# Moving the transfers of SyncE's queue to GpSimd in a streaming adjacency matmul with residual and layernorm

## The reference, cut to what matters

```
def _L0_gnn_ref(X, A_hat, w, W_agg):
    agg = A_hat @ (X @ W_agg)
    aggregated_term = w[:, None] * jax.nn.relu(agg)
    residual_term = (1.0 - w)[:, None] * X
    return aggregated_term + residual_term
x = _layernorm(x + _L0_gnn_ref(x, adj, w, W_agg), axis=-1)   # eps 1e-05
```

## Time and profile before

| | |
|---|---|
| median of 3 runs | 638.72 us (638.65 to 639.68) |
| profiled execution, its own time | 638.89 us |
| its span, first to last instruction | 637.0 us |
| mean granted TensorE clock | 0.912 |
| busy: PE, DVE, ACT, POOL | 519.5, 55.8, 15.9, 0.3 us |
| DMA packets | 272.75 MB, mean 428 GB/s over the span |

### The profile page before, as it was taken

The page is one execution under the profiler, slowest core; times in us unless marked ns, Lnnn a source line. Parts: engine busy times, 40 slices in busy tenths (PEclk is TensorE's granted clock), DMA queues, the critical chain, the costliest instruction groups (busy, mean ns, idle before and its releaser), DMA issues.

```text
span 637.0 us, 5371 instructions
## 1 busy us (share of the span) xinstructions
PE 519.5 (82%) x2304; PEld 177.2 (28%) x2304; DVE 55.8 (9%) x136; ACT 15.9 (2%) x35; POOL 0.3 (0%) x5
## 2 busy tenths in 40 slices
PE   0678798878987888797878977878887987978996
PEld 0123232222222322222222322322222222222345
DVE  2000101010010100101001010100101001010102
ACT  0000000000000000000000000000000000000000
POOL 0000000000000000000000000000000000000000
PEclk9997898888979889897988979898888989888999
DMA  9999999999999999999999999999999999999998
GB/s 362 453 418 453 419 427 433 425 447 428 444 414 447 419 429 443 441 432 419 451 410 436 436 450 423 427 431 425 446 424 453 424 429 419 436 444 420 428 413 349
DMA packets 9667, 272.75 MB, mean 428 GB/s; under 512 B 1472, under 2 KB 1728, under 8 KB 3008
## 3 DMA queue, kind: packets, MB, share of 16 engines
q1 hardware_dynamic: 9360, 272.63, 99.6%
q10 hardware_dynamic: 304, 0.07, 0.1%
HBM read 270.60 MB, written 2.10 MB: 428 GB/s over the span
## 4 chain that ended last, share of the span: by engine, by line
DMA 69%; PE 29%; issue 0%; SPq 0%; ACT 0%; DVE 0%; DVEq 0%
DMA ring<-adj_main_dram 69%; PE bank L156 29%; PE bank L164 0%; SPq L114 0%; ACT aggT L203 0%; ACT aggT L208 0%; SPq L110 0%; SPq L109 0%; DVE res L267 0%; ACT std_last L199 0%; DVE y_last L261 0%; ACT aggT L211 0%; DVE stats L263 0%; DVE y_last L262 0%; DVE mv L264 0%
## 5 line engine op out<-in xcount | busy, mean ns | idle before, releaser
L156 PE MATMUL bank<-ring,x_sb 128*64 128x512 f32 (+2 forms) x2176 | 501.7, 621 | 102.2 <-DMA ring<-adj_main_dram 102.1
L156 PEld LDWEIGHTS bank<-ring,x_sb 128*64 128x64 f32 x2176 | 161.6, 148 | 430.2 <-issue 299.7
L245 DVE SCALAR_TENSOR_TENSOR y<-bank,w_sb 128x256 f32<-128x256 f32 (+1 forms) x16 | 6.7, 420 | 552.7 <-PE bank L164 552.7
L164 PE MATMUL bank<-wagg,aggT 128*128 128x64 f32 x128 | 17.9, 281 | 11.2 <-ACT aggT L203 10.3
L164 PEld LDWEIGHTS bank<-wagg,aggT 128*128 128x128 f32 x128 | 15.6, 191 | 25.4 <-ACT aggT L203 23.5
L203 ACT COPY aggT<-bank 128x512 f32<-128x512 f32 x15 | 8.8, 585 | 527.0 <-PE bank L156 527.0
L234 DVE TENSOR_TENSOR y<-y,res 128x256 f32<-128x256 f32 (+1 forms) x16 | 6.7, 420 | 2.2
L242 DVE TENSOR_TENSOR res<-y,rstd 128x256 f32 (+1 forms) x16 | 6.7, 421 | 0.6
L238 DVE TENSOR_TENSOR sq<-y 128x256 f32<-128x256 f32 (+1 forms) x16 | 6.7, 421 | 0.6
L236 DVE SCALAR_TENSOR_TENSOR y<-rowsum,y 128x256 f32<-128x256 f32 (+1 forms) x16 | 6.7, 420 | 0.5
L239 DVE TENSOR_REDUCE varsum<-sq 128x4 f32<-128x256 f32 (+1 forms) x16 | 6.7, 416 | 0.5
(11 more groups left out here) (9 smaller groups left out, 1.3 us busy)
## 6 DMA issues: line engine op xcount, KB each, us to landing
ring<-adj_main_dram SPq DMA_DIRECT2D x30, 5632.0 KB, 27.2
ring<-adj_main_dram SPq DMA_DIRECT2D x15, 5120.0 KB, 29.8
ring<-adj_mid_dram SPq DMA_DIRECT2D x2, 2304.0 KB, 22.8
ring<-adj_mid_dram SPq DMA_DIRECT2D x1, 3072.0 KB, 21.5
ring<-adj_mid_dram SPq DMA_DIRECT2D x2, 1536.0 KB, 23.9
x_sb<-x_dram SPq DMA_DIRECT2D x1, 2048.0 KB, 8.0
out_dram<-res SPq DMA_DIRECT2D x1, 2016.0 KB, 8.1
ring<-adj_last_dram SPq DMA_DIRECT2D x2, 768.0 KB, 23.0
```

The lines of the kernel that those rows point to most:

```text
L156: last = nc.tensor.matmul(into[j % 2 * D:(j % 2 + 1) * D, 0:cols], x_sb[:, j], ring[:, at + s * cols:at + (s + 1) * cols], start=j < 2, st ...
L164: last = nc.tensor.matmul(rows[:, i * D:(i + 1) * D], aggT[:, i * P:(i + 1) * P], wagg2[:], start=True, stop=True)
L245: step(nc.vector.scalar_tensor_tensor(out=y[:, 0:n], in0=rows.rearrange("p (n d) -> p n d", d=D), scalar=0.0, in1=over_row(w_sb[:, bass.ds ...
```

## The change

All transfers of SP's program are issued by GpSimd, in the same order and with the same waits, behind the memset of `eps`. SP's program is gone. The stores get a semaphore each (`stored`, `rows_stored`), so ScalarE ends with two waits for 16 in place of one for 32. The loads of W_agg and the last store stay on ScalarE.

```
-        @block.sync
-        def _(sp):
-            sp.dma_start(x_sb[:], x.rearrange("(p t) d -> p t d", p=P)).then_inc(x_in, 16)
-            sp.dma_start(w_sb[:], w.rearrange("(p t) -> p t", p=P)).then_inc(w_in, 16)
+        @block.gpsimd
+        def _(pool):
+            nc.gpsimd.memset(eps[:], EPS).then_inc(eps_ready, 1)
+            pool.dma_start(x_sb[:], x.rearrange("(p t) d -> p t d", p=P)).then_inc(x_in, 16)
+            pool.dma_start(w_sb[:], w.rearrange("(p t) -> p t", p=P)).then_inc(w_in, 16)
...
-            with sp.Fori(1, G) as g:
+            with pool.Fori(1, G) as g:
                 for c in range(C):
-                    sp.wait_ge(slot_free, g * C + (c + 1 - C))
+                    pool.wait_ge(slot_free, g * C + (c + 1 - C))
                     main_load(c, adj_main[bass.ds(g, 1), 0])
...
-            sp.wait_ge(out_ready, LAST)
-            sp.dma_start(out_rows[:, 0:LAST_T0], res[:, 0:LAST_T0]).then_inc(stored, 16)
-
-        @block.gpsimd
-        def _(pool):
-            nc.gpsimd.memset(eps[:], EPS).then_inc(eps_ready, 1)
+            pool.wait_ge(out_ready, LAST)
+            pool.dma_start(out_rows[:, 0:LAST_T0], res[:, 0:LAST_T0]).then_inc(rows_stored, 16)
...
-            act.wait_ge(stored, 2 * 16)
+            act.wait_ge(stored, 16)
+            act.wait_ge(rows_stored, 16)
```

More of the change, by code:

```diff
@@ L102, in gnn_residual_layernorm @@
         out_ready = sem("out_ready")
-        stored = sem("stored")
+        stored, rows_stored = sem("stored"), sem("rows_stored")
         out_rows = out.rearrange("(p t) d -> p t d", p=P)
         block = ctx.enter_context(nc.Block())
-        @block.sync
-        def _(sp):
-            sp.dma_start(x_sb[:], x.rearrange("(p t) d -> p t d", p=P)).then_inc(x_in, 16)
-            sp.dma_start(w_sb[:], w.rearrange("(p t) -> p t", p=P)).then_inc(w_in, 16)
+        @block.gpsimd
[3 more added lines that the diff above has]
+            pool.dma_start(w_sb[:], w.rearrange("(p t) -> p t", p=P)).then_inc(w_in, 16)
             def main_load(c, load):
                 j, n = sum(MAIN_LOADS[:c]), MAIN_LOADS[c]
-                sp.dma_start(ring[:, c * SLOT:c * SLOT + n * COLS], load[:, :, j:j + n].rearrange("o q s n -> (o q) (s n)")
+                pool.dma_start(ring[:, c * SLOT:c * SLOT + n * COLS], load[:, :, j:j + n].rearrange("o q s n -> (o q) (s n)")
                              ).then_inc(loaded[c], 16)
@@ L128, in _ @@
                     freed += 1
-                    sp.wait_ge(slot_free, (G - 1) * C + freed)
-                sp.dma_start(ring[:, j * MID_COLS:(j + n) * MID_COLS],
+                    pool.wait_ge(slot_free, (G - 1) * C + freed)
+                pool.dma_start(ring[:, j * MID_COLS:(j + n) * MID_COLS],
                              adj_mid[0, :, j:j + n].rearrange("q s n -> q (s n)")).then_inc(mid_loaded[k], 16)
                 j += n
-            sp.wait_ge(slot_free, G * C)
+            pool.wait_ge(slot_free, G * C)
             j = 0
             for k, n in enumerate(LAST_LOADS):
-                sp.dma_start(ring[:, LAST_AT + j * P:LAST_AT + (j + n) * P],
+                pool.dma_start(ring[:, LAST_AT + j * P:LAST_AT + (j + n) * P],
                              adj_last[:, j:j + n].rearrange("q s n -> q (s n)")).then_inc(last_loaded[k], 16)
                 j += n
-            sp.wait_ge(out_ready, LAST)
-            sp.dma_start(out_rows[:, 0:LAST_T0], res[:, 0:LAST_T0]).then_inc(stored, 16)
-        @block.gpsimd
-        def _(pool):
-            nc.gpsimd.memset(eps[:], EPS).then_inc(eps_ready, 1)
+            pool.wait_ge(out_ready, LAST)
+            pool.dma_start(out_rows[:, 0:LAST_T0], res[:, 0:LAST_T0]).then_inc(rows_stored, 16)
         @block.tensor
```

## The result

The changed kernel takes 642.49 us (642.23 to 643.46, 4 runs) against 639.17 us (638.65 to 639.68, 4 runs) of the kernel before, a ratio of 1.0055 with an interval of 1.0043 to 1.0067: 3.5 us slower, between 2.7 and 4.3 us. The profiled execution took 642.34 us, 3.45 us more than the profiled one of before.

A forecast was written before the change was run, and what follows sets the result against it. The prediction took the transfer rate, 432 GB/s, as the bound. It added 0.1 us (memset), 0.6 us (first transfer) and 0.1 us (end) to 638.89 us, giving 639.7, stated as 639.6 us; range 638.0 to 645.0 us.

The forecast's parts named there:

- The end: Close of the program: one more wait on ScalarE and retiring POOL's transfers add 0.1 us, at most 1.9 us.
- (a): Rival at the start: POOL's first transfer or first few are slow, time about 641 us; chance 0.21.
- (b): Rival over the whole span: the same bytes move more slowly, 6.3 us per 1% of rate, 645 us; chance 0.13.
- (c): Rival in the last main slot: TensorE's clock is lower for part of it, +1.6 us, about 641; chance 0.06 alone.
- The first transfer: Start of the program: x waits 0.1 us behind POOL's memset and takes 0.6 us longer to its first byte.
- The covered issues: Later loads at the start, in the loop and at the end: queued transfers hide POOL's slower issue, cost nothing.
- The late store: Store after VectorE's last instruction: late engines set its landing, so nothing is added, or 0.2 us if they start later.
- The lock between VectorE and POOL: POOL's transfers wait for descriptors while VectorE runs a two-port mode: taken as nothing, needing 12 us in one piece.
- (d): Rival over the whole span: the transfer rate rises, 0.5% being 3.1 us, time 636.6 us; chance 0.10.

## Why the prediction was right, and where it was not

The time lies in the range of 638.0 to 645.0 us, and the sign was held possible with 0.4, but the forecast itself, 639.6 us and no measurable change, was not met. The step that failed is "The end". That the time lies in the range all the same is luck: the range reached up to 645.0 for the rivals (a), (b) and (c), and none of them made the time. The signs that the prediction named for its forecast came true: the first byte moves at 2.7 us, the middle has 432 GB/s, a group takes 38.8 us in the chain (ring loads at 136.94 and 175.73 us), and POOL's store lands within 0.3 us of ScalarE's. None of these signs looked behind the last landing.

**The end.** I put it at +0.1 us and its bound at 1.9 us, by doubling what lies outside the span now. It is 2.6 us in the span, above the bound. The wait on ScalarE is no part of that, as the run with only the ring loads on POOL has the same two waits. The step spoke of POOL's transfers "to be retired", without asking for each how many there are. The runs give the price, with 0.1, 1.4, 2.6, 2.7 and 4.0 us behind the landing of the store for 1, 33, 63, 65 and 97 transfers: (4.0 - 0.1)/96 = 41 ns for each. POOL's DRAIN in the kernel before stands behind no transfer at all, and SP's took 0.12 us behind 65, so no row of before could have priced this, and my bound was not tied to the number of transfers.

**The first transfer.** The sum was 0.1 + 0.6 us; the start measures 0.94 us at the last contraction. The memset is not a term (0.02 us when moved). POOL shows x at 1.41 instead of 0.74 us; 0.12 us of that is only a later start of all engines against the first instruction (ScalarE's first issue is at 0.86 instead of 0.74 us); outside the span 0.15 us are gained, about as much. From issue to first byte it is 1.3 to 1.4 us, 0.3 to 0.4 more than SP's 1.0. The Trainium skill (DMA: Bandwidth & Descriptors, Latency and other measured facts) has about 1 µs and 600 ns there: both traces are 0.3 to 0.4 us above it, and its difference of 0.4 agrees with them. The half microsecond ahead of the issue comes on top of that here.

**The covered issues.** Right. A ring load takes POOL 527 ns where SP took 333, all 42 inside the loop, and the window of the middle still has 432 GB/s. The nine loads of the last part were out by 608.3 us, sooner than the 612 us of the prediction, at 527 to 541 ns each. That the ring loads on POOL are free was shown by the run that has only them there.

**The late store.** Right in the mechanism: the late engines set its landing. It landed 1.4 us later than before, 0.5 us more than the 0.9 us that everything is late; with the 0.37 us of slack that makes 0.1 us exposed, where I took nothing. In the run with the memset moved, VectorE was 1.5 us later and the store still landed at 630.89 + 6.7 = 637.6 us.

**The lock between VectorE and POOL.** No run tested it by itself. The rows show no trace of it. POOL's 45 main loads took 527 to 530 ns, all of them. That alone says little, since VectorE works for 55.8 us in 640. The run with 32 small transfers says more: POOL issued them without a pause from 4.2 to 19.4 us, and about nine fall inside VectorE's longest instruction. None took longer than 499 ns:

```profile
L115 POOL DMA_DIRECT2D ring<-adj_main_dram x45: 527/527/530, 2.6 to 563.6; - x45
...
L123 POOL DMA_DIRECT2D tiny<-w_dram x32: 484/484/499, 4.2 to 18.9; - x32
...
10.12 4.42 DVE L232 TENSOR_TENSOR res<-x_sb,two_minus_w 128x4096 f32<-128x4096 f32 x1
```

The first row is of the changed kernel, the other two of the run with 32 small transfers. Whether that instruction runs in one of the modes that the prediction names no run shows, so the lock is not refuted; it has no price in this kernel.

**The rivals.** (a) had the right sign and nearly the right size for a wrong reason: the first transfer was not slow enough. (b) and (d) are out, the rate is the same with both queues; the run with only the ring loads on POOL leaves at most 0.05% above the kernel before. (c) exists and can fall either way from one execution to the next. The kernel before itself has two groups, 24 of the 43 executions that stand beside the experiments at 638.55 to 639.09 us and 19 at 639.39 to 640.47 us; that these are the two sides of (c) is inferred from the few executions that were profiled. In the profile of the ring-only kernel the last third slot fell on the slow side; its window and its row in the timeline, and the row of the kernel before:

```profile
591.88:602.40 10.52, 10.50 (x40) 3.19 (x40) 0.00 (x0) 0.00 (x0) 0.00 (x0) 0.84 1.00 426
...
591.88 10.50 PE L156 MATMUL bank<-ring,x_sb 128*64 128x512 f32 x40 [2.46 <-DMA ring<-adj_main_dram]
...
591.95 8.80 PE L156 MATMUL bank<-ring,x_sb 128*64 128x512 f32 x40 [0.77 <-DMA ring<-adj_main_dram]
```

Its granted clock is 0.84, 1.2 GHz for part of it, against 1.00 in the earlier trace rows. Ahead of it TensorE had stood idle for 2.46 us, ahead of the fast one for 0.77 us. That profiled execution took 639.96 us, 1.1 us over its median. In the changed kernel the slow slot is hidden, which I had not seen: the moved-memset run had it (10.5 us, last contraction at 627.25 instead of 625.74 us) and its profiled execution took 642.34 us, as the changed kernel's did with the fast slot. There the end is set by the store and the drain behind it.

## What to carry to other kernels

A large transfer can be issued by GpSimd for free if others are queued ahead of it, and not if it is the first of the program: that cost 0.9 us here. What has to be counted is the number of transfers that GpSimd has issued in the whole program: in these runs, with 1 to 97 of them, 41 ns for each stood behind the landing of its last one, and 83 ns when it waited for that landing itself. So the last transfer of a program belongs on another engine's queue when GpSimd has issued many; GpSimd can then drain while that one is under way. And an end that the chain doesn't explain is looked for in the instructions that count as no work.

## What the runs showed of the hardware

- The closing DRAIN of GpSimd has a price for every transfer that the program issued there, long landed ones too: 41 ns behind the last landing, the same for 16 rows of 8 bytes as for 128 rows of 44 KB. SP's closing DRAIN took 0.12 us behind 65 transfers.
- Short rows come in fewer packets from GpSimd's queue: 8736 in place of 9360 for the same bytes, and the 624 that are gone are all packets under 8 KB (2384 in place of 3008). The stretch of 612 to 618 us moved at 412 instead of 403 GB/s; the time did not profit, as TensorE is in the chain there.
- 32 transfers of 128 bytes in one queue between large ones kept the engines from other work for 0.14 us each. In a queue of their own beside the large ones they did not; the last stores landed 1.0 to 1.2 us later there than in the kernel before, for a reason that is not shown.
- GpSimd's first transfer of a program shows as an instruction about 0.5 us after the engine could begin (1.39 us against 0.86 us for ScalarE's first), with a memset ahead of it or not.
